# Cross attention on one core: the first scores round and the last value projection move between slots, and two tiles change engines

## What is computed

```python
# layer 0: no mask, no biases; layer 1: mask, biases, scale 1/sqrt(16)
q = split_heads(layernorm(x) @ Wq)       # 16 heads of 16, 64 queries a sequence
k = split_heads(ctx @ Wk)                # 1601 keys
v = split_heads(ctx @ Wv)
scores = einsum('bhqd,bhkd->bhqk', q, k) (+ mask * -1e9)
attn = softmax(scores)
x = x + merge_heads(einsum('bhqk,bhkd->bhqd', attn, v)) @ Wo
```

## Time and profile before

| | before |
|---|---|
| median of 3 runs | 2327.14 us (2322.26 to 2331.49) |
| the profiled execution | 2325.12 us, span 2323.3 us |
| TensorE busy | 2062.7 us, 89% of the span |
| VectorE busy | 1335.3 us, 57% |
| ScalarE busy | 1105.0 us, 48% |
| GpSimd busy | 459.7 us, 20% |

### The profile page before, as it was taken

How to read it: one execution, slowest core, us unless ns; L and a number is a source line. 1 busy time by engine, 2 the same in 40 slices (tenths; PEclk the granted TensorE clock), 3 DMA queues, 4 the chain that set the end, 5 groups by cost and what they waited for, 6 DMA issues and landing times. The chain is left out here.

```text
span 2323.3 us, 59919 instructions
## 1 busy us (share of the span) xinstructions
PE 2062.7 (89%) x25136; PEld 1575.4 (68%) x25136; DVE 1335.3 (57%) x3546; ACT 1105.0 (48%) x2109; POOL 459.7 (20%) x367
## 2 busy tenths in 40 slices
PE   6999999999999985588997899999999999987874
PEld 4777777777777763267995677777777777764553
DVE  3566666566666656935114366666666666563685
ACT  4555555555554543521333554555455554551681
POOL 3111122221111100210001333222233332200010
PEclk9999999999999997797998999999999999996867
DMA  4111111111111001003653221122111111100000
GB/s 127 30 30 30 30 30 40 39 41 30 30 30 30 7 2 55 1 9 127 218 200 99 53 53 44 45 53 61 44 53 47 52 44 45 31 2 22 1 1 25
DMA packets 68668, 110.93 MB, mean 48 GB/s; under 512 B 14505, under 2 KB 37170, under 8 KB 68402
## 3 DMA queue, kind: packets, MB, share of 16 engines
q1 hardware_dynamic: 68402, 107.10, 15.7%
HBM read 106.04 MB, written 1.05 MB: 46 GB/s over the span
## 5 line engine op out<-in xcount | busy, mean ns | idle before, releaser
L718 DVE CUSTOM_DVE_ANT_0 maps_d<-scores_d,mask_scaled_d 128x512 f32<-128x512 f32 (+1 forms) x512 | 263.5, 571 | 217.3 <-PE scores_d L519 217.3
L718 DVE CUSTOM_DVE_ANT_0 maps_a<-scores_a,no_mask_a 128x512 f32<-128x512 f32 (+1 forms) x512 | 263.5, 571 | 214.0 <-PE scores_a L519 214.0
L529 PE MATMUL turn_a<-const,maps_a 128*128 128x128 f32 (+1 forms) x1664 | 258.7, 282 | 16.5 <-DVE mapsT_a L746 15.7
L529 PE MATMUL turn_d<-const,maps_d 128*128 128x128 f32 (+1 forms) x1664 | 258.8, 282 | 16.2 <-DVE mapsT_d L746 15.4
L636 ACT ACTIVATE mapsT_d<-turn_d 128x512 f32<-128x512 f32 x224 | 129.6, 595 | 231.8 <-PE turn_d L529 231.7
L636 ACT ACTIVATE mapsT_a<-turn_a 128x512 f32<-128x512 f32 x224 | 129.6, 595 | 231.2 <-PE turn_a L529 231.1
L529 PEld LDWEIGHTS turn_a<-const,maps_a 128*128 128x128 f32 (+1 forms) x1664 | 184.0, 142 | 74.2 <-issue 25.1
L529 PEld LDWEIGHTS turn_d<-const,maps_d 128*128 128x128 f32 (+1 forms) x1664 | 184.1, 142 | 74.0 <-issue 25.1
L641 ACT ACTIVATE maps_a<-maps_a,neg_max_a 128x1024 f32<-128x1024 f32 (+1 forms) x256 | 222.5, 953 | 1.9 <-DVE neg_max_a L725 1.9
L641 ACT ACTIVATE maps_d<-maps_d,neg_max_d 128x1024 f32<-128x1024 f32 (+1 forms) x256 | 222.5, 953 | 1.9 <-DVE neg_max_d L725 1.9
L746 DVE COPY mapsT_a<-turn_a 128x512 f32<-128x512 f32 x192 | 129.8, 685 | 76.7 <-PE turn_a L529 76.3
(11 more groups left out here) (412 smaller groups left out, 4396.8 us busy)
## 6 DMA issues: line engine op xcount, KB each, us to landing
w_c<-in_L_ffn_W SPq DMA_DIRECT2D x30, 1024.0 KB, 6.8
raw_a<-in_ctxT SPq DMA_DIRECT2D x48, 512.0 KB, 3.7
raw_d<-in_ctxT SPq DMA_DIRECT2D x48, 512.0 KB, 3.7
mask_scaled_d<-in_mask SPq DMA_DIRECT2D x32, 400.2 KB, 5.4
raw_a<-in_ctxT SPq DMA_DIRECT2D x16, 65.0 KB, 3.0
raw_d<-in_ctxT SPq DMA_DIRECT2D x16, 65.0 KB, 7.0
x<-in_x SPq DMA_DIRECT2D x1, 1024.0 KB, 5.4
Wk_c_b<-in_L_attn_Wk_c SPq DMA_DIRECT2D x1, 1024.0 KB
```

Of the source, the lines that this page charges most:

```text
L529: ins = nc.tensor.transpose(TP[at % 2][0:r, P * j:P * j + P], maps[g % 2][:, j, P * t:P * t + r], chip.ident)
L718: nc.vector.tensor_tensor_reduce(maps[b][:, j, cols], SC[j][:, 0:w], mf[m % 2][:, cols] if masked else none[:, 0:w], 1.0, NEG, ALU.add, AL ...
```

## The change

Five edits, all within `cross_by_rows` and its tables.

1. Round 0 of scores, with its four maxima, leaves slot 0. In slot 12 (`NEXT_ROUND_AT`) of half g TensorE does round 0 of half g + 2, behind turn 12 and ahead of values 10 and 11. Round 0 of group 1 is issued ahead of the loop. Each round's maxima wait for the turns of half g - 2 that read the columns they overwrite (up to 4, 8, 12, 13 turns) in place of one wait at chunk 0.
2. The last value projection of a sequence's half moves from slot 12 (even halves) and slot 9 (odd halves) to slot 11.
3. Tiles 11 and 12 are moved by ScalarE. It does the eight exponentials between tile 6 and tile 11. The value copy of slot 11 is ScalarE's too.
4. `spread_sums` and `finish` go from slot 9 to slot 10.
5. In slot 10 TensorE issues `spread_sums` ahead of the projection. VectorE's `finish` stays last in its slot: behind the move of tile 10 and the key copy.

```diff
-V_AT = [{3: 0, 6: 1, 9: 2, 12: 3}, {3: 4, 6: 5, 9: 6}]
-ROUND_AT = {0: 0, 2: 1, 4: 2, 6: 3}
-SUM_AT = 9
-LATE = 7
+V_AT = [{3: 0, 6: 1, 9: 2, 11: 3}, {3: 4, 6: 5, 11: 6}]
+ROUND_AT = {2: 1, 4: 2, 6: 3}
+NEXT_ROUND_AT = KT - 1
+SUM_AT = 10
+BY_DVE = range(7, 11)
+BY_ACT = [t for t in range(KT) if t not in BY_DVE]
@@ TensorE
             pe.wait_ge(project_free, len(FIRST))
+            scores(1, 0)
             for g in range(GROUPS):
@@
                     if t in ROUND_AT and g + 1 < GROUPS:
                         scores(g + 1, ROUND_AT[t])
+                    if t == NEXT_ROUND_AT and g + 2 < GROUPS:
+                        scores(g + 2, 0)
+                    if t == SUM_AT and g:
+                        spread_sums(g - 1)
                     if t in K_AT and m + 1 < NB:
                         k_unit(m + 1, 4 * h + K_AT[t])
                     if t in V_AT[h] and m + 1 < NB:
                         v_unit(m + 1, V_AT[h][t])
-                    if t == SUM_AT and g:
-                        spread_sums(g - 1)
@@ ScalarE
-                for t in range(LATE):
+                for t in BY_ACT:
+                    if t == BY_DVE.stop and g + 1 < GROUPS:
+                        for i in range(8):
+                            exp(g + 1, i // 4, i % 4)
                     move(g, t)
@@
-                if g + 1 < GROUPS:
-                    for i in range(8):
-                        exp(g + 1, i // 4, i % 4)
@@ VectorE
                 if chunk == 0 and j == 0:
                     if masked and g % 2 == 0:
                         dve.wait_ge(mask_ready, m + 1)
-                    after(dve, turned, KT * (g - 1))
                 if j == 0:
+                    after(dve, turned, KT * (g - 2) + min(BANK // P * (chunk + 1), KT))
                     dve.wait_ge(scored, 4 * g + chunk + 1)
@@
+            for j in range(4):
+                largest(1, 0, j)
             for g in range(GROUPS):
                 m, h = g // 2, g % 2
                 for t in range(KT):
-                    if t >= LATE:
+                    if t in BY_DVE:
                         move(g, t)
+                    if t == NEXT_ROUND_AT and g + 2 < GROUPS:
+                        for j in range(4):
+                            largest(g + 2, 0, j)
```

More of the change, by code:

```diff
@@ L294, in round_order @@
     order = [("score", 0, c, j) for c in range(4) for j in range(4)]
+    order += [("score", 1, 0, j) for j in range(4)]
     for g in range(GROUPS):
@@ L298, in round_order @@
                 order += [("score", g + 1, ROUND_AT[t], j) for j in range(4)]
+            if t == NEXT_ROUND_AT and g + 2 < GROUPS:
+                order += [("score", g + 2, 0, j) for j in range(4)]
             if t == SUM_AT and g:
@@ L373, in wait_moved @@
                 g, t = at // KT, at % KT
-                if t < LATE:
-                    eng.wait_ge(moved_act, LATE * g + t + 1)
+                if t in BY_DVE:
+                    eng.wait_ge(moved_dve, len(BY_DVE) * g + t - BY_DVE.start + 1)
                 else:
-                    eng.wait_ge(moved_dve, (KT - LATE) * g + t - LATE + 1)
+                    eng.wait_ge(moved_act, len(BY_ACT) * g + BY_ACT.index(t) + 1)
         def key_columns(chunk):
@@ L809, in _ @@
                             negate(g + 1)
-                    if t >= LATE and t in K_AT and m + 1 < NB:
+                    if t in BY_DVE and t in K_AT and m + 1 < NB:
                         keep_k(m + 1, 4 * h + K_AT[t])
-                    if t >= LATE and t in V_AT[h] and m + 1 < NB:
+                    if t in BY_DVE and t in V_AT[h] and m + 1 < NB:
                         keep_v(m + 1, V_AT[h][t])
```

## The result

The changed kernel took 2230.2 us (median of 4 runs, 2228.5 to 2237.5) where the kernel before took 2327.3 (2322.3 to 2331.5): a ratio of 0.959, interval 0.956 to 0.962. The forecast was 2237 us and 0.961. The profiled execution took 2230.6 us with a span of 2228.8; before 2325.1 and 2323.3. So 94.5 us left the span.

The account below looks back on a forecast made before the run. TensorE was taken as the bound. Per stage, 43.3 us from the loop plus 3.0 from the last pair less 1.1 make 45.2, twice 90.4; 2325.1 becomes 2234.7, and 2.0 for the median gives 2237 us (2224 to 2250).

Parts of the forecast that it names:

- Even half: Half with four value projections: 13.81 us from turn 0 to turn 7, then 11.62 us to the next turn 0.
- Odd half: Half with three value projections: 13.81 us from turn 0 to turn 7, then 9.35 us to the next turn 0.
- Loops: Fifteen pairs of halves with projections in each cross attention stage, each 2.89 us shorter: 43.3 us a stage.
- Ends: Each stage outside the fifteen pairs: scores ahead of the loop cost 1.07 us, last pair gains 3.0 (bounds 0 and 4.2).
- The new wait: Last pair, without projections: ScalarE's tiles 11 and 12 stand behind exponentials ending after turn 11; eats part of the gain.
- the slow stretch: Last pair: the new wait could bring TensorE's 1.2 GHz clock or not, about 1.4 us a stage either way.
- Margin of ScalarE in odd halves: Tile 12's copy ends 8.8 us behind turn 7, its values are issued at 9.1: margin 0.3 us.
- VectorE's extra waits: A wait added ahead of each scores round for turns finished long before: bounds 0 and 0.10 us, taken as 0.
- GpSimd "priced at nothing": GpSimd's context splits, SyncE's loads behind them and masks wanted one slot earlier were expected to cost nothing.
- 1 (a wait stays): Rival: the moved round only shifts its wait, or turn 12 still waits; 2250 to 2290 us, chance 0.12.
- 2 (ScalarE becomes the bound): Rival: exponentials end L late, odd halves lose L - 0.3, even L - 2.6; slower from L = 2.9 us; chance 0.03.
- 3 (the bank): Rival: the 2.89 us are lost again at the projections' bank in slots 10 and 11; time within 0.5%, chance 0.05.

Follow-up runs that it names:

- The last kernel: Changed kernel, but in half 30 alone VectorE moves tiles 11 and 12 and does finish behind them: 2226.4 us, ratio 0.957.
- the mask held back: Changed kernel with last value projections back in slots 12 and 9, and GpSimd waiting for finish before scaling the mask: 2242.1 us, ratio 0.965.
- the doses: Changed kernel with extra ScalarE copies behind each half's exponentials: three of 577 columns 2269.1 us (ratio 0.976), nine of 230 columns 2314.7 us (0.995).

## Why the prediction was right

Point by point:

- **Even half** 25.43 forecast, 25.43 measured. Slot 10's projection starts 323.28 - 317.33 = 5.95 us behind turn 7, turn 2 to round 1 is 306.38 - 305.85 = 0.53, turn 12 to scores 0.53, scores 1.07, values 0.81: each of these terms of the sum is back in a row of its own. **Odd half** 23.16 forecast, 23.14 measured. Turns 9 and 10, taken from the middle of their bounds as 0.50 + 0.49, take 346.76 - 345.77 = 0.99; the sums, taken as 0.39, take 347.12 - 346.76 = 0.36. The method carried this: starts to starts from places where nothing held the step, rather than busy shares.
- **Loops** 43.3 us a stage forecast; 43.3 in stage a, 44.1 in stage d, whose odd halves were some 0.04 us longer before the change, one of them 0.4.
- **Ends.** I took +3.0 for the last pair and -1.07 for the scores ahead of the loop. The last pair gave 20.95 - 20.25 = 0.7 in half 30 and 15.06 - 12.96 = 2.1 from the last half's first turn to its last sums, 2.8 in all (2.7 in stage d). The new wait came as told (2.71 us), and with it the slow stretch: 2.59 us for three turns, against 2.91 in the earlier trace rows. The granted clock was 0.50 from 808.3 to 809.3 us and back at 1.00 from 811.9 on. This is the point on which I had not put a sign. The Trainium skill (TensorE: Matmul & The Clock Gate, Part 1) has the slow clock as the default, which activity releases; the trace agrees here too. The last kernel takes this wait away and the slow stretch goes with it. The loop's first turn comes 1.94 us later than before, 1.07 of it the scores.
- **What was missed.** Two stages of (43.3 + 2.8 - 1.1) and (44.1 + 2.8 - 1.1) make 90.8 of the 94.5 us; the rest, some 4 us, lies in stages that the change doesn't touch. From the last sums of the first cross attention to the first turn of the second it is 1.2 us less, though 1.07 us of scores were added there; behind the second it is 2.4 us less; ahead of the first loop it is 0.9 us more than the scores. Such differences are within what these stretches show from one profile to another (see the mask held back), so they are no merit of the forecast and no fault of it. With the median's distance from the profiled run (-0.4 in place of the 2.0 of before) this is the 7 us between forecast and result.
- **Margin of ScalarE in odd halves** 0.3 forecast, 0.76 measured. The term most mis-sized is the value copy, put at 0.6 us like a tile: in the row of 350.08 it takes 0.37 and tile 12 starts 0.27 behind it, having 256 columns and not 512. That is 0.33 of the 0.46 us. Tile 11, put at 0.6 as well, holds the next copy back for 0.47 (350.08 - 349.61), another 0.13.
- **VectorE's extra waits** taken at 0 within 0 to 0.10; the price is 0.11 a round, just outside, and it costs nothing in the loop for the reason given, 4.10 us between rounds 1 and 2 where 3.99 are needed.
- **GpSimd "priced at nothing"** was right in number and wrong in reasoning. I looked at who waits for GpSimd, not at what its work does to VectorE's. In stage d the mask scaling comes within 1.0 us of `finish`, and the move of one value projection, whose place I took for free before that run, is what keeps them apart. Had it stayed, the result would have been 2278 us and outside my range. No rival of mine had this mechanism, so on this point the forecast was right by luck.
- **Rivals.** 1 (a wait stays): no wait for maxima or tiles stays in the thirty halves. 2 (ScalarE becomes the bound): the mechanism is real and the doses price it, but it decides at more than L = 2.9 us. From L - 0.76 and L - 2.6 a pair is slower than before where 2L - 3.36 exceeds 2.89, from L = 3.1, a little less where the clock falls too. 3 (the bank): this is what happens with the sums in slot 9, where key copy and value copy are both late; in slot 10 it doesn't.

## What to carry to other kernels

Where one engine is busy above 95% with its clock full, write the new order anew from start-to-start prices of steps that nothing holds, and then ask of each other engine when its result is there; here that gave each half to 0.02 us. Parts of a reordering need not add up: a step moved into a gap can be the very cover that another move needs (39 and 23 us alone, 94 together), so price them in company. And look for any long GpSimd instruction that could come to lie beside VectorE's work from SBUF to SBUF: compare least, median and most of each small instruction's durations, since nothing is listed as a wait.

## What the runs showed of the hardware that I had not expected

- A VectorE tensor_scalar on 128x64 with all operands in SBUF took 4.14 us (else 0.31) beside a GpSimd tensor_scalar of 4.32 us on 128x1601 that had started 0.22 us earlier, fourteen times out of fourteen; a tensor_tensor beside GpSimd's q_rows took 0.43 us where it takes 0.30. The maxima, which read scores from PSUM and a mask from SBUF, kept their 0.69 us beside the same mask scaling in the changed kernel (it runs from 1441.86 and slot 12's maxima from 1442.14).
- A semaphore wait long met cost VectorE 0.11 us a round of four maxima.
- ScalarE's copies follow one another faster than their durations say: a tile's copy of 0.58 us let the next instruction start after 0.47 (350.08 - 349.61), and a 65x256 copy of 0.37 us after 0.27.
- Behind waits of 1.1 and 0.3 us in a loop that is otherwise full, the granted clock fell to 0.50 for part of the next half in every second even half from half 8 on, in both stages; behind the same waits it stayed at 1.00 in the others. Why these and not those, no run here tells.
